# Gate and up products of the experts: rounded parts in steps 10 to 13 only, plain fp32 elsewhere

## The reference

```python
def _expert_ffn(x, w1, wg, w2):
    return jax.nn.silu(x @ w1) * (x @ wg) @ w2

output = _expert_ffn(x, Ws1, Wsg, Ws2)                 # the shared expert
...                                                    # softmax gate, the 3 best of 7 experts
for e in range(NUM_ROUTED):                            # 7
    w_e = jnp.sum(topk_probas * (topk_idxs == e), axis=-1)
    output = output + _expert_ffn(x, W1[e], Wg[e], W2[e]) * w_e[..., None]
```

## Time and profile before

| | |
|---|---|
| median of 3 runs | 481.17 us (481.15 to 482.25) |
| the profiled execution, first to last instruction | 480.6 us |
| PE busy | 379.6 us, 79% |
| DVE busy | 356.3 us, 74% |
| ACT, POOL busy | 164.5 us, 163.9 us, 34% each |

### The profile page before, as it was taken

How to read it: one execution, slowest core, us unless ns; L and a number is a source line. 1 busy time by engine, 2 the same in 40 slices (tenths; PEclk the granted TensorE clock), 3 DMA queues, 4 the chain that set the end, 5 groups by cost and what they waited for, 6 DMA issues and landing times. The chain is left out here.

```text
span 480.6 us, 6802 instructions
## 1 busy us (share of the span) xinstructions
PE 379.6 (79%) x2360; PEld 257.9 (54%) x2360; DVE 356.3 (74%) x833; ACT 164.5 (34%) x239; POOL 163.9 (34%) x168
## 2 busy tenths in 40 slices
PE   7899789999999758976882999996856289850764
PEld 3476456645567647865651677774633066530333
DVE  4488348576646999699979477589995955689895
ACT  4356525324322212522350333332006344240331
POOL 4009800058434455555334233243412120030240
PEclk9899998599999879999996899999789569976687
DMA  8900000022301222303976920790000760000001
GB/s 279 262 20 1 10 1 2 0 70 74 98 22 44 87 88 64 111 7 108 220 174 109 155 88 2 116 170 1 1 1 29 134 78 2 2 0 0 23 16 51
DMA packets 33713, 32.67 MB, mean 68 GB/s; under 512 B 3876, under 2 KB 32784, under 8 KB 33680
## 3 DMA queue, kind: packets, MB, share of 16 engines
q1 hardware_dynamic: 31088, 28.99, 26.7%
q0 software_dynamic: 992, 1.68, 1.1%
q10 hardware_dynamic: 1600, 1.57, 1.0%
HBM read 28.04 MB, written 4.19 MB: 67 GB/s over the span
## 5 line engine op out<-in xcount | busy, mean ns | idle before, releaser
L913 PE MATMUL bank<-tok_r,probs_r 128*128 128x512 f32 x104 | 47.5, 457 | 24.6 <-DVE silu_sb L1511 10.2
L939 PE MATMUL bank<-wexp,wT 128*128 128x256 f32 x192 | 53.5, 405 | 4.9 <-DVE x L1528 4.8
L1202 ACT ACTIVATE silu_sb<-bank 128x512 f32<-128x512 f32 x32 | 19.1, 597 | 88.2 <-PE bank L913 88.2
L705 POOL TENSOR_TENSOR wexp_r<-wexp,probs_r 128x1024 fp32r<-128x1024 f32 x13 | 31.0, 2382 | 50.0 <-ACT probs_r L1163 50.0
L603 POOL TENSOR_TENSOR mx_grid<-parts,bl 128x1024 bf16<-128x1024 fp8e4 x9 | 17.2, 1908 | 84.3 <-DVE parts L1720 84.3
L1395 DVE TENSOR_SCALAR probs<-probs,hi 128x512 f32<-128x512 f32 x64 | 34.8, 597 | 15.0 <-ACT probs L1152 14.9
L939 PEld LDWEIGHTS bank<-wexp,wT 128*128 128x128 f32 x192 | 37.0, 202 | 11.9 <-issue 6.6
L1152 ACT ACTIVATE probs<-bank 128x1024 f32<-128x1024 f32 x32 | 32.3, 1026 | 31.4 <-PE bank L825 31.3
L913 PE MATMUL bank<-tok_r,wexp_r 128*128 128x512 f32 x104 | 42.4, 407 | 0.0
L913 PEld LDWEIGHTS bank<-tok_r,probs_r 128*128 128x128 f32 x104 | 20.8, 200 | 31.9 <-issue 14.3
L825 PE MATMUL bank<-qrep,krep 32*128 32x256 f32 x256 | 35.6, 409 | 2.1 <-ACT probs L1152 1.1
(11 more groups left out here) (275 smaller groups left out, 881.6 us busy)
## 6 DMA issues: line engine op xcount, KB each, us to landing
wexp<-in_L_ffn_W SPq DMA_DIRECT2D x28, 256.0 KB, 4.5
krep<-part_dram SPq DMA_DIRECT2D x32, 128.0 KB, 6.1
qrep<-part_dram SPq DMA_DIRECT2D x32, 128.0 KB, 4.9
wexp<-in_L_ffn_Wg SPq DMA_DIRECT2D x14, 256.0 KB, 4.5
part_dram<-parts POOLq DMA_DIRECT2D x4, 384.0 KB, 3.0
part_dram<-parts SPq DMA_DIRECT2D x4, 384.0 KB, 3.2
x<-in_x ACTq DMA_DIRECT2D x2, 512.0 KB, 7.1
ctx<-in_ctx SPq DMA_DIRECT2D x2, 512.0 KB, 7.0
```

The lines of the kernel that those rows point to most:

```text
L705: gp.tensor_tensor(low, raw, w_high[k % 2].bitcast(F32), ALU.subtract).then_inc(s["w_low_ready"], 1)
L913: mm = pe.matmul(bank[:, bk, :], lhs, rhs, start=(kk == 0 and q == 0), stop=(kk == KC - 1 and q == len(terms) - 1))
L939: mm = pe.matmul(bank[:, 2 + pair, D * t:D * t + D], hid[k % 2][m][:, col:col + P], wexp[:, k % WR, 2, m, :], start=(m == 0), stop=(m == 1))
L1202: act.activation(silu_sb[:, w % 2, :], bank[:, 0, :], ACT.Silu if direct else ACT.Tanh, scale=1.0 if direct else 0.5).then_inc(s["sigmoid_ ...
```

## The change

The rounded parts are used only in steps 10 to 13 (`SPLIT_STEPS`), which are all of half 1. Steps 3 to 9, 14 and 15 use plain fp32 products as steps 0 to 2 do. The weight splits of those nine steps go, on ACT and on POOL, with PE's waits for them, and so does the token split of half 0. The low part of the tokens of half 1 gets a place of its own (`x_low`, over the last parts of the context) instead of `xnT`, because steps 8, 9, 14 and 15 now read `xnT` whole.

```diff
--- before.py
+++ after.py
@@ -89,7 +89,7 @@
     return (4, 5) if w < 16 else (w % 3, 3 + w % 3)
 
 
-SPLIT_FROM = 3
+SPLIT_STEPS = range(10, 14)
 
 
 SILU_STEPS = (3, 4, 5, 6, 7, 8, 14, 15)
@@ -153,13 +153,13 @@
     plan += end[0] + end[1] + st("project", 4) + end[2] + st("project", 5) + end[3] + end[4] + st("project", 6) + end[5]
     plan += st("delta_in", 0) + st("delta_root", 0) + st("project", 7) + st("v_project", 2, 3) + st("score", 16, 17)
     plan += st("delta_mid", 0) + st("delta_out", 0) + st("score", 18, 19) + st("ln_in", 2) + st("score", 20, 21) + st("ln_root", 2)
-    plan += st("ln_out", 2) + st("score", 22, 23) + st("clamp", 16, 17, 18, 19) + st("xt", 0) + st("route", 0) + st("x_split", 0)
+    plan += st("ln_out", 2) + st("score", 22, 23) + st("clamp", 16, 17, 18, 19) + st("xt", 0) + st("route", 0)
     rest = [st("values", 4) + st("clamp", 20, 21) + st("values_copy", 4) + st("route_rank", 0), st("clamp", 22, 23) + st("route_weigh", 0)]
 
     def expert(k, mx=None):
 
         now = st("gate", 2 * k) + st("up", 2 * k)
-        if SPLIT_FROM < k + 1 < 2 * NX:
+        if k + 1 in SPLIT_STEPS:
             now += st("w_split", k + 1)
         if k:
             now += st("out", 2 * k - 2)
@@ -177,7 +177,6 @@
 
 
     plan += weave(flat([expert(k) for k in range(3)]), rest + attention(6, 4) + attention(7, 4) + attention_end(7))
-    plan += st("w_split", 3)
     chain = st("delta_in", 1) + st("delta_root", 1) + st("delta_mid", 1) + st("delta_out", 1) + st("ln_in", 3) + st("ln_root", 3) + st("ln_out", 3)
     plan += weave(expert(3, 0) + expert(4, 1) + expert(5, 2), chain)
     plan += weave(expert(6, 3), st("xt", 1) + st("route", 1)) + st("x_split", 1) + weave(expert(7, 4), st("route_rank", 1) + st("route_weigh", 1))
@@ -391,13 +390,10 @@
 
         probs_r = sb_rounded("probs_r", [P, 2, HC, 2 * S], "probs")
         tok_r = sb_rounded("tok_r", [P, NT, D], "tok")
-        parts_r = sb_rounded("parts_r", [P, KC, HALF], "parts")
-        xnT_r = sb_rounded("xnT_r", [P, KC, NT * P], "xnT")
         wexp_r = sb_rounded("wexp_r", [P, WR, 3, KC, D], "wexp")
         w_high = [probs_r[:, q, :, 384:512] for q in range(2)]
-        x_high = [tok_r[:, TH * n:TH * n + TH, :].rearrange("p i d -> p (i d)").rearrange("p (c t) -> p c t", c=KC)
-                  for n in range(2)]
-        x_low = [parts_r[:, :, :], xnT_r[:, :, HALF:2 * HALF]]
+        x_high = tok_r[:, TH:NT, :].rearrange("p i d -> p (i d)").rearrange("p (c t) -> p c t", c=KC)
+        x_low = nc.alloc_sbuf_tensor_at("x_low", [P, KC, HALF], F32R, offset=place["parts"] + 2 * 3 * HALF * 2)
 
         bank = ctx_.enter_context(nc.psum_tensor("bank", [P, 8, 512], F32))
 
@@ -662,16 +658,13 @@
                 gp.tensor_tensor(parts[:, u, 2, :], rest, parts[:, u, 1, :], ALU.subtract).then_inc(s["kl1"], 1)
                 gp.wait_ge(s["kl1"], u + 1)
                 gp.dma_start(part_dram[1, u].rearrange("a p t -> p a t"), parts[:, u, :, :]).then_inc(s["ck_stored"], 16)
-            def x_split(n):
-
-                gp.wait_ge(s["x_high_ready"], n + 1)
-                gp.wait_ge(s["logits_done"], n + 1)
-                if n == 0:
-                    gp.wait_ge(s["ck_stored"], 16 * 4)
-                gp.tensor_tensor(x_low[n], xnT[:, :, HALF * n:HALF * n + HALF], x_high[n].bitcast(F32),
+            def x_split(_):
+
+                gp.wait_ge(s["x_high_ready"], 1)
+                gp.wait_ge(s["ck_stored"], 16 * 4)
+                gp.tensor_tensor(x_low[:, :, :], xnT[:, :, HALF:2 * HALF], x_high.bitcast(F32),
                                  ALU.subtract).then_inc(s["x_low_ready"], 1)
 
-            x_split(0)
             gp.wait_ge(s["gate_loaded"], 16 * 14)
             seq.wait()
             for j in range(2):
@@ -699,7 +692,7 @@
                                  ctx[:, i, :].rearrange("p (h v) -> p h v", v=HD), 1.0, 1.0, ALU.mult, ALU.mult).then_inc(s["ctx_v_placed"], 1)
             def w_split(k):
 
-                gp.wait_ge(s["w_high_ready"], k - SPLIT_FROM + 1)
+                gp.wait_ge(s["w_high_ready"], k - SPLIT_STEPS[0] + 1)
                 raw = wexp[:, k % WR, 0:2, :, :].rearrange("p j c d -> p (j c d)").rearrange("p (q o) -> p q o", o=P)
                 low = wexp_r[:, k % WR, 0:2, :, :].rearrange("p j c d -> p (j c d)").rearrange("p (q o) -> p q o", o=P)
                 gp.tensor_tensor(low, raw, w_high[k % 2].bitcast(F32), ALU.subtract).then_inc(s["w_low_ready"], 1)
@@ -735,7 +728,7 @@
 
             steps = dict(w_split=w_split, x_split=x_split, mx_grids=mx_quantise, q_split=q_split, state=state, cell_in=cell_in, quantise=quantise)
             for name, i in plan:
-                if name in steps and (name, i) != ("x_split", 0):
+                if name in steps:
                     steps[name](i)
 
 
@@ -903,12 +896,12 @@
                 claim(bk, reader, count)
                 for kk in range(KC):
                     weight = wexp[:, k % WR, bk, kk, P * m:P * m + P]
-                    if k < SPLIT_FROM:
+                    if k not in SPLIT_STEPS:
                         terms = [(weight, xnT[:, kk, HALF * n:HALF * n + HALF])]
                     else:
                         high = w_high[k % 2][:, 4 * bk + 2 * kk + m, :]
                         low = wexp_r[:, k % WR, bk, kk, P * m:P * m + P]
-                        terms = [(high, x_high[n][:, kk, :]), (high, x_low[n][:, kk, :]), (low, x_high[n][:, kk, :])]
+                        terms = [(high, x_high[:, kk, :]), (high, x_low[:, kk, :]), (low, x_high[:, kk, :])]
                     for q, (lhs, rhs) in enumerate(terms):
                         mm = pe.matmul(bank[:, bk, :], lhs, rhs, start=(kk == 0 and q == 0),
                                        stop=(kk == KC - 1 and q == len(terms) - 1))
@@ -920,9 +913,9 @@
                 pe.wait_ge(s[f"wg_loaded{k % WR}"], 32 * (k // WR + 1))
                 if k % (NE + 1) == 0:
                     pe.wait_ge(s["xt_evacuated"], 2 * (k // (NE + 1)) + 2)
-                if k >= SPLIT_FROM:
-                    pe.wait_ge(s["w_low_ready"], k - SPLIT_FROM + 1)
-                    pe.wait_ge(s["x_low_ready"], k // (NE + 1) + 1)
+                if k in SPLIT_STEPS:
+                    pe.wait_ge(s["w_low_ready"], k - SPLIT_STEPS[0] + 1)
+                    pe.wait_ge(s["x_low_ready"], 1)
                 half_hidden(w, 0, *(("sigmoid_done", w + 1) if k in SILU_STEPS else ("silu_ready", tanh_steps(w))), "a_done")
 
             def up(w):
@@ -1155,9 +1148,9 @@
             def w_split(k):
 
                 act.wait_ge(s[f"wg_loaded{k % WR}"], 32 * (k // WR + 1))
-                if k == SPLIT_FROM:
+                if k == SPLIT_STEPS[0]:
                     act.wait_ge(s["pv_done"], 8)
-                if k - 2 >= SPLIT_FROM:
+                if k - 2 in SPLIT_STEPS:
                     act.wait_ge(s["b_done"], 2 * (k - 2) + 2)
                 raw = wexp[:, k % WR, 0:2, :, :].rearrange("p j c d -> p (j c d)").rearrange("p (q o) -> p q o", o=P)
                 act.activation(w_high[k % 2], raw, ACT.Copy).then_inc(s["w_high_ready"], 1)
@@ -1165,7 +1158,7 @@
             def x_split(n):
                 act.wait_ge(s["xt_turned"], 2 * n + 2)
                 act.wait_ge(s["xt_evacuated"], 2 * n + 2)
-                act.activation(x_high[n], xnT[:, :, HALF * n:HALF * n + HALF], ACT.Copy).then_inc(s["x_high_ready"], 1)
+                act.activation(x_high, xnT[:, :, HALF * n:HALF * n + HALF], ACT.Copy).then_inc(s["x_high_ready"], 1)
 
             def values_copy(g):
                 act.wait_ge(s["pv_done"], g + 1)
```

## The result

The changed kernel takes 467.48 us (median of 4 runs, 465.75 to 468.84); beside it, on the same chip, the kernel before took 481.16 us (4 runs, 478.11 to 482.25). The ratio is 0.9715, with a 95% interval of 0.9671 to 0.9759. The forecast was 470.2 us, in a range of 466.5 to 477. The profiled execution of the changed kernel has a span of 463.9 us, against 480.6 before. These two are the fastest run of the one kernel (465.75 us) and the slowest of the other (482.25 us), so their difference, 16.7 us, is larger than that of the medians, 13.7 us.

The account below looks back on a forecast made before the run. DVE was taken to pace steps 3 to 9, 14 and 15, PE steps 11 to 13. 480.6 - 10.1 - 0.9 = 469.6 us profiled, plus 0.6 for the median: 470.2 us, range 466.5 to 477.

Parts of the forecast that it names:

- fp32 costs PE 0.70 us per half: Nine unrounded steps: a half takes 5.16 us instead of 4.46, 1.40 us more per step, 12.6 us more PE work.
- POOL's subtractions hold DVE up by 10.5 us: Steps 5 to 9: DVE instructions stretched to the end of POOL's subtraction lose 10.5 us in all.
- The replay up to step 10: From 146 us, following PE and DVE: step 10's gate starts at 226.6 instead of 236.7 us, 10.1 us early.
- The split of step 10 costs 1.4 us: Step 9 to 10: the remaining split meets DVE at line 1295, costing 1.4 us instead of 2.0.
- No DVE instruction over 1.5 us up to 215 us: Sign in the changed profile: between 146 and 215 us no DVE instruction exceeds 1.5 us.
- the first rival: DVE instructions meet POOL's quantising at up to five places, 1 us each: 5 us back, 475.2 us; chance 0.22.
- Steps 10 to 13 unchanged: From 237 to 320 us nothing changes but the split of step 14; the stretch moves as a whole.
- Steps 14 and 15: 0.9 us: Ends 0 or 1.8 us early, depending on the lower clock in the last two halves; 0.9 taken, half way.
- After 350: 0, within 1.5 us: After 350 us order and durations stay: 0, within 1.5 us for where the lower clock level falls.
- The range: Given 466.5 to 477 us: low end adds 0.5 for the tail, high end is the first rival plus 2 us.
- Another cause for DVE's long instructions: Rival: not POOL but something else stretches DVE, so DVE-paced stretches do not move: 480 to 482 us; chance 0.05.
- A slower PE clock: Rival, 172 to 223 us: lower clock uses up 4 us of slack; 38 us of it give about 485 us; chance 0.07.

Follow-up runs that it names:

- without subtractions: Kernel before, POOL skipping the weight subtractions of steps 3 to 9 and PE multiplying the high part again: 467.51 us, ratio 0.9694.
- idle splits: Changed kernel with the weight splits of steps 3 to 9 kept on ACT and POOL, waited for but unused: 478.93 us, ratio 0.9948.
- second pair: Changed and unchanged kernels measured again without edits: changed 468.48 us, ratio 0.9735; unchanged 480.6 and 481.93 us, one run each.

## Why the prediction was right

- **fp32 costs PE 0.70 us per half.** Right: a half takes 5.16 us. PE's busy time in steps 3 to 9 rises by 4.92 us only. That this is not 9.8 fits with the clock, which the prediction passed over here: in the kernel before part of PE's busy time was at the lower level (0.94 against 1.00 now). Between the runs without subtractions and with idle splits, both at 0.96, it is 81.14 - 72.72 = 8.42 us; what the last 1.4 us are, no run shows. The Trainium skill has four passes for an fp32 product (FP8 and Floating Point Precision, TensorE Precision Notes). The prediction took a rounded pass for one of them and had 0.92 us; but 2.92 / 12 is 0.243 us and not 0.23, which makes 0.97. The profile after has 3.43 / 4 = 0.86 us again, 0.215 us for each of four. That does not speak against the four passes, only against the length of a rounded one as theirs.
- **POOL's subtractions hold DVE up by 10.5 us.** Right: 10.98 us of busy time in the profiles, 10.33 in the run without subtractions alone. It is the term that carries the result, and two runs show it from either side (80.97 us with the subtractions left out, 90.33 with them kept).
- **The replay up to step 10.** The prediction had step 10's gate 10.1 us early. The stretch is 9.44 us shorter, and step 3 no longer waits the 0.45 us of the earlier trace rows for its split: 9.9. (The replay starts the step at 145.4; 146.02 - 0.45 is 145.6, which changes nothing of weight.) The time of that gate on the profile's scale, 223.88 us where 226.6 was forecast, adds the 2.8 us that were there before step 3. The single waits came much as drawn: PE's before the out of step 4 is 2.00 us (forecast 2.4, before 4.85), DVE's wait for Silu is 2.36 us as before, PE's idle time 2.97 us (forecast 4).
- **The split of step 10 costs 1.4 us.** Right in size, 1.39 us, on line 1286 (1293 in the kernel before) and not, as forecast, on 1295.
- **No DVE instruction over 1.5 us up to 215 us.** It holds, narrowly: 1.48 us on line 1442. With 1.36 on line 1328 and 1.03 on line 1494 these are the meetings with POOL's quantising that the first rival spoke of. The rival's 5 us did not come: the run without subtractions and the change have the stretch within 0.3 us, and DVE got all its 10.5 us back.
- **Steps 10 to 13 unchanged.** 0.3 us shorter. But the clean line between a stretch that DVE paces and one that PE paces was too coarse. In the early part of it the split of step 11 cost DVE 3.7 us, and the runs with fewer rounded steps show that rounding steps 10 and 11 brings nothing: four rounded steps take 164.94 us, none 164.39, and only two 162.28.
- **Steps 14 and 15: 0.9 us.** Mis-sized: 1.57 us, near the end of 1.8. The prediction took half way because the last two halves follow a long wait at the lower clock level and could take it back. They didn't. The wait is 3.56 us now and was 4.66: the fp32 work goes into the wait. The kernel before took 26.57 us at a mean clock of 0.87 and 26.55 at 0.94, so this difference in PE's clock doesn't show in the stretch. DVE sets it. From 324.40 us (after: 311.88) to the end of step 15 DVE waits for nothing, 22.85 us before and 20.70 after; the difference, 2.15 us, is that of line 1549. Ahead of that it starts 0.58 us later, behind the slower first `up`. 2.15 - 0.58 = 1.57 us is the whole difference; the prediction had these two terms, 2.1 and 0.6, and then took less for the last halves. PE's wait of 1.78 us for the split ran beside a busy DVE and is worth nothing by itself.
- **After 350: 0, within 1.5 us.** It was 2.0 us shorter in the profiled execution, outside the 1.5, and 3.4 us came before step 3, 0.45 of them the wait that went. After step 15 nothing was edited; before step 3 the token split of half 0 and the weight split of step 3 went. But the changed kernel also began step 3 at 145.90 us, where the kernel before has 145.81 to 146.71, and the repetitions move each of the two stretches by about 3 us. The steps of the change sum to 0.45 + 9.44 + 0.3 + 1.57 = 11.8 us. The medians differ by 13.7 (13.5 in the second pair), against which the prediction had 11.0. The last 1.9 us are smaller than what the clock does in single executions. But the run without subtractions fell by more than its stretch as well (14.4 against 9.7 us), so whether a shorter middle also makes the clock fall less often stays open.
- **The range.** That the median lies inside it is partly luck. The terms that the prediction gives, 12.2 and 1 us below 481.2, are 468.0 and not 467, and with the 0.5 us for the tail 467.5, which is where the measured 467.48 lies. The stated 466.5 had 1 us more room than its own sum.
- **The other rivals.** Another cause for DVE's long instructions fell with the run without subtractions. A slower PE clock didn't come: it was 1.00 through steps 3 to 9, where PE worked 78.27 of 81.24 us, against 0.94 before, where it had longer waits.
- **What was missed.** That four rounded steps are too many. The price per split was in the earlier trace rows for the steps up to 9; the prediction did not cost the scan of step 11 in the same way.

## What to carry to other kernels

Before moving work to an idle engine, look for instructions on the bound engine that end together with that engine's: here nine subtractions on POOL, 21.4 us, cost DVE 12.8 us (10.98 and 1.85 us of busy time in the two stretches), and 16% more matmul time per half (5.16 against 4.46 us) was the cheaper way. Ask it again for every stage, since here the rounded parts paid in steps 12 and 13, where PE is the bound, and not in 3 to 11. When small differences count, cut both profiles at the same events and run the unchanged kernel again, to see which stretches repeat.

## What was unexpected in the hardware

**Very small instructions wait in full.** A `TENSOR_SCALAR` on 4 values per partition takes 0.16 us and took 2.33 beside a subtraction on POOL; on int32 0.17 and 1.56; on 16 values of uint32 0.17 and 1.12, in the two kernels shown above. In these cases the DVE instruction ends with POOL's, so the loss is as long as what POOL has left and not as the DVE instruction. A scan of 64x256 went from 0.68 to 2.73 us.

**Either engine can be the loser.** In the kernel before, timelines of POOL and DVE:

```profile
338.89 1.22 DVE L1691 TENSOR_TENSOR pvs<-pvs,arows 128x1024 f32<-128x1024 f32 x1
339.03 2.22 POOL L590 TENSOR_TENSOR mxraw<-mxraw,mx_grid 128x512 f32<-128x512 f32 x1
340.15 2.19 DVE L1693 TENSOR_TENSOR x<-x,pvs 128x1024 f32<-128x1024 f32 x1
```

DVE was first, and POOL's instruction, which takes 1.27 us at the least and 1.29 in the median, took 2.22; the next one of DVE then started 1.10 us before POOL was done and took 2.19 us, where the one before it, of the same size, took 1.22. The lengths fit with each waiting for the other's end.

**The clock's falls aren't the same each time.** In the same program, over 15 us that begin with the same work, PE was granted 0.77 of its clock in one execution and 0.98 in another. That moved single stretches by about 3 us in 480.
